# First attention of a graph network kernel: values weighed four slots at a time instead of two

## The chip, the cores and the metric

The kernel runs on one core of one Trainium2 chip. The metric is the device time of one execution in microseconds (us); the kernel before was run three times and the median counts. Beside these runs there is one execution recorded by the hardware profiler, from which all rows below come.

## The reference

Four layers of a graph network over 6250 nodes of 256 features and 106250 edges, each with a layer norm and a residual. The change touches the first one, a dot-product attention over the edges:

```
h = max(layernorm(x), 0)
q, k, v = h @ Wq + bq, h @ Wk + bk, h @ Wv + bv       # 8 heads of 32
scores = sum(q[src] * k[dst], over a head) / sqrt(32)
e = exp(scores - max of the scores of the same dst)
out = segment_sum(v[src] * e / sum(e), by dst)
x = x + out
```

The other three layers (a gated graph layer, a relational convolution with 8 edge types, an attention with additive scores and a batch norm) are not touched.

## The kernel before

Edges are sorted by destination and cut into slots of 128 edges, one edge to a partition; a slot's edges all end in one tile of 128 nodes. There are 880 slots, worked on in 55 iterations `j` of a ring of 16 slots (`RING`), each in two halves `h` of 8 slots (`GROUP`). One half is called a group here: 110 groups.

`dot_attention` is the stage of the first attention. Each engine has its own program, and they meet at semaphores only. For each group:

- GpSimd gathers for each slot the rows of its sources (`gather`, L729): per edge 256 numbers of q and then 8 heads of 32 values plus one place for the weight, 33 numbers a head. A slot of the ring is gathered anew once its sum is done.
- TensorE multiplies the transposed one-hot matrices of two slots (a pair, q = 0 to 3) with the keys of the node tile (`keys_of`, L961), which gives each edge the key of its destination. VectorE multiplies it with the q part of the rows, in place (`multiply_keys`, L1108, 512 numbers on each partition), and after four pairs sums them by head to scores (`sum_scores`, L1113).
- TensorE turns the scores (`turn_scores`, L969 and L970), VectorE scans them for running maxima by destination (`scan_within` L1121, `join_slots` L1128 to L1136, `scan_across` L1143 and L1145), with short steps of TensorE between (`row_of_ends` L979, `spread_bounds` L984, `lowered_node` L998 and L999, `differences` L990 and L991). ScalarE takes the exponential and writes the weights into the 33rd places (`weights_of`, L1079).
- VectorE weighs the values with them, in place (`weigh_values`, L1160, 2 slots x 8 heads x 32 = 512 numbers).
- TensorE sums a slot's values and weights by destination with the one-hot matrix (`sums_of`, which calls `aggregate`, L764), and VectorE adds the sum to the node tile's (`add`, which calls `accumulate`, L771). `lower_sums` (L1152) scales the running sums by the fall of the maximum.

TensorE also computes fillers (`keep_busy`, `keep_warm`, L862), whose results nobody reads; six of them stand before `turn_scores`.

The order on each engine is written out by hand in `on_vector` and `on_tensor`: in the loop over groups, group g is weighed and summed while the keys and scores of group g + 1 (`more`) are computed, and the one-hots of group g + 2 (`later`) are turned. An instruction that waits holds back all behind it on its engine. The semaphores around the change: `weight_ready` (weights written), `msg_ready` (values weighed, counted in pairs, eight to an iteration), `agg_done` (a slot summed), `acc_done` (a slot's sum added), `key_ps` and `pair_used` (keys of a pair computed, and used). The two helpers that sums and additions go through wait like this:

```python
def aggregate(pe, j, b, at, width, banks=(6, 7)):
    pe.wait_ge(acc_done, now(j, b - len(banks), RING))
    nc.tensor.matmul(psum[:, banks[b % len(banks)], 0:width], oh[:, b // GROUP, b % GROUP],
                     rows[:, b, at:at + width], start=True, stop=True).then_inc(agg_done, 1)

def accumulate(dve, j, b, place, width, banks=(6, 7), sums=acc):
    dve.wait_ge(agg_done, now(j, b, RING))
    dve.wait_ge(acc_done, now(j, b - 1, RING))
```

In this stage there are four banks for the sums. A matmul of 32-bit numbers shows as two instructions in the trace, so four L764 are the sums of two slots and four L961 the keys of one pair.

Of the kernel before, what the change touches and what calls it, by code (L numbers as in the profile page):

```python
# [18 lines left out]
ALU, ACT, AX = mybir.AluOpType, mybir.ActivationFunctionType, mybir.AxisListType  # L19
# [3 lines left out]
P = 128  # L23
N, D, HEADS, DH, RELS, EDGES = 6250, 256, 8, 32, 8, 106250
# [57 lines left out]
def build(nc, ctx, a, out):  # L82
# [3 lines left out]
    def sem(name):  # L86
        return ctx.enter_context(nc.semaphore(name))
# [65 lines left out]
    def landed(use):  # L153

        return 16 * (use + 2)
# [8 lines left out]
    def now(i, p, n=2):  # L166


        return n * i + p + n + 1
# [591 lines left out]
# [9 lines that stand above are left out]
        to = at_place(sums, place, width)  # L770
        nc.vector.tensor_tensor(to, to, psum[:, banks[b % len(banks)], 0:width], ALU.add).then_inc(acc_done, 1)  # L771
# [8 lines left out]
    shifted, weight_ready, msg_ready = sem("shifted"), sem("weight_ready"), sem("msg_ready")  # L780
# [83 lines left out]
    def dot_attention():  # L864
# [51 lines left out]
        def nth(j, h):  # L916

            return 2 * j + h + 1

        def group_rows(h):  # L920
            return rows[:, h * GROUP:(h + 1) * GROUP, :]

        def value_heads(h):
            return group_rows(h)[:, :, vat:vat + ACCW].rearrange("p s (h d) -> p s h d", d=HW)
# [76 lines left out]
        def sums_of(pe, j, h, slots):  # L1001
            pe.wait_ge(wide_ready, nth(j, h))
            for s in slots:
                if s % 2 == 0:
                    pe.wait_ge(msg_ready, now(j, 4 * h + s // 2, 8))
                aggregate(pe, j, h * GROUP + s, vat, ACCW, banks)

        def on_tensor(pe):
# [94 lines left out]
        def multiply_keys(dve, j, h, q):  # L1103
            for b in range(2):
                dve.wait_ge(ring[h * GROUP + 2 * q + b], landed(j))
            dve.wait_ge(key_ps, now(j, 4 * h + q, 8))
            pair = group_rows(h)[:, 2 * q:2 * q + 2, 0:D]
            nc.vector.tensor_tensor(pair, ps_pair(q).rearrange("p (s f) -> p s f", s=2), pair,  # L1108
                                    ALU.mult).then_inc(pair_used, 1)

        def sum_scores(dve, j, h):
            dve.wait_ge(pair_used, now(j, 4 * h + 3, 8))
            nc.vector.tensor_reduce(score[h].rearrange("p (h s) -> p s h", s=GROUP),  # L1113
                                    group_rows(h)[:, :, 0:D].rearrange("p s (h d) -> p s h d", h=HEADS),
                                    axis=AX.X, op=ALU.add).then_inc(score_ready, 1)
# [36 lines left out]
            c.step(nc.vector.scalar_tensor_tensor(acc0, ps_alpha.unsqueeze(2).to_broadcast([P, HEADS, HW]), 1.0, acc0,  # L1152
                                                  ALU.add, ALU.mult))

        def weigh_values(dve, j, h, q):
            if q == 0:
                dve.wait_ge(weight_ready, now(j, h))
            pair = value_heads(h)[:, 2 * q:2 * q + 2]
            val = pair[:, :, :, 0:DH]
            nc.vector.tensor_tensor(val, val, pair[:, :, :, DH:].to_broadcast([P, 2, HEADS, DH]),  # L1160
                                    ALU.mult).then_inc(msg_ready, 1)

        def add(dve, j, h, s, places):
            accumulate(dve, j, h * GROUP + s, places[s], ACCW, banks)

        def begin(dve, c):
            v = nc.vector
            dve.wait_ge(sums_clear, 1)
            for h in range(2):
                c.step(v.memset(by_link(link[h][:, 0:HEADS * LINK])[:, :, 0], -BIG))  # L1170
                c.step(v.memset(link[h][:, HEADS * LINK:], -BIG))
                c.step(v.memset(padded[h], 0.0))
                c.step(v.memset(breaks16[h][:, P:], 0.0))
            c.step(v.memset(bound[1], -BIG))
            c.step(v.memset(minus, -1.0))
            c.step(v.tensor_copy(flipped, ident[:, ::-1]))
            c.step(v.tensor_copy(paired[:, 0::2], ident[:, GH:]))
            c.step(v.tensor_copy(paired[:, 1::2], ident[:, 0:GH]))
            c.step(v.tensor_scalar(negated, ident[:, 0:GH], -1.0, None, ALU.mult))
            c.then(v.tensor_copy(ident16, ident[:, :]))  # L1180
            dve.sem_inc(begun, 1)

        def on_vector(dve):
            c = v_own.bind(dve)
            begin(dve, c)
            for q in range(4):
                multiply_keys(dve, 0, 0, q)
            sum_scores(dve, 0, 0)
            scan_within(dve, 0, 0)
            join_slots(dve, c, 0, 0)  # L1190
            scan_across(dve, c, 0, 0)
            multiply_keys(dve, 0, 1, 0)
            places = acc_places(slot(0, 0), GROUP)
            for g, (j, h) in enumerate(groups):
                more, later = at(g + 1), at(g + 2)
                lower_sums(dve, c, j, h, places[0])
                weigh_values(dve, j, h, 0)
                c.wait()
                if more:
                    multiply_keys(dve, *more, 1)  # L1200
                weigh_values(dve, j, h, 1)
                weigh_values(dve, j, h, 2)
                add(dve, j, h, 0, places)
                if more:
                    multiply_keys(dve, *more, 2)
                weigh_values(dve, j, h, 3)
                add(dve, j, h, 1, places)
                add(dve, j, h, 2, places)
                if more:
                    multiply_keys(dve, *more, 3)  # L1210
                    sum_scores(dve, *more)
                add(dve, j, h, 3, places)
                add(dve, j, h, 4, places)
                if more:
                    scan_within(dve, *more)
                add(dve, j, h, 5, places)
                if more:
                    join_slots(dve, c, *more)
                add(dve, j, h, 6, places)
                if more:  # L1220
                    scan_across(dve, c, *more)
                add(dve, j, h, 7, places)
                if later:
                    multiply_keys(dve, *later, 0)
                if more:
                    places = acc_places(slot(*more), GROUP)
            dve.wait_ge(acc_done, now(ITERS - 1, RING - 1, RING))
# [1541 lines left out]
```

## Time and profile before

| | us |
|---|---|
| median of three runs | 8025.69 |
| lowest and highest run | 8011.5 and 8032.68 |
| profiled execution, its time | 8034.18 |
| profiled execution, span from first to last instruction | 8031.9 |
| TensorE busy (matmuls) | 6812.9 (85%) |
| VectorE busy | 5413.0 (67%) |
| GpSimd busy | 4516.3 (56%) |
| ScalarE busy | 1518.2 (19%) |

The profile page gives busy times over the whole span, with stages that have different limits. The first attention is the stretch from about 600 to 2170 us. PE is TensorE (PEld its weight loads), DVE VectorE, ACT ScalarE, POOL GpSimd. PEclk is the granted TensorE clock as a share of full speed: 1.00 is 2.4 GHz, 0.50 is 1.2 GHz, and a value between is a mean over the stretch. The rows of the trace that are used stand in the section after the change.

### The profile page before, as it was taken

How to read it: one execution, taken by the hardware profiler on the slowest of the kernel's cores; microseconds unless marked ns; L12 is line 12 of the kernel's file. 1: busy time of each engine (PE TensorE's matmuls, PEld its weight loads, DVE VectorE, ACT ScalarE, POOL GpSimd, SP SyncE). 2: the span in 40 equal slices, each digit the busy share in tenths (PEclk: the TensorE clock that was granted, in tenths of full speed). 3: DMA queues.
4: the chain of work that ended last, by engine and by line, in shares of the span. 5: the costliest groups of instructions: out<-in, count | busy, mean ns of one | idle time of the engine just before them, and what ended most of it. 6: DMA issues, size and time to landing. Idle time of an engine off the chain costs nothing. (4 is left out here: it accounts for less than half of the span.)

```text
span 8031.9 us, 101344 instructions
## 1 busy us (share of the span) xinstructions
PE 6812.9 (85%) x30971; PEld 3926.6 (49%) x30971; DVE 5413.0 (67%) x12509; ACT 1518.2 (19%) x4812; POOL 4516.3 (56%) x4616
## 2 busy tenths in 40 slices
PE   1379999999859999899999999989999868888883
PEld 1136666666535444455555544444444444444442
DVE  8788999999876666644444444444444488888887
ACT  0021111111110000000000045500000044444441
POOL 1005555555457777777777711167777636666660
PEclk9999999999979999999999999999999999999997
DMA  0256666666643333354444544433333444444443
GB/s 8 56 204 174 173 172 171 173 172 173 165 133 101 96 98 98 99 118 135 131 130 132 135 146 162 162 114 104 103 105 103 103 142 115 114 114 113 114 110 99
DMA packets 462335, 1016.96 MB, mean 127 GB/s; under 512 B 114227, under 2 KB 229471, under 8 KB 455158
## 3 DMA queue, kind: packets, MB, share of 16 engines
q0 software_dynamic: 240960, 702.53, 32.7%
q1 hardware_dynamic: 220854, 308.06, 11.9%
q8 instruction: 258, 4.23, 0.2%
q14 instruction: 263, 2.15, 0.1%
HBM read 849.27 MB, written 160.73 MB: 126 GB/s over the span
## 5 line engine op out<-in xcount | busy, mean ns | idle before, releaser
L764 PE MATMUL psum<-rows,oh 128*128 128x257 f32 (+2 forms) x8800 | 2708.4, 406 | 362.8 <-DMA rows<-h_tab,src_i 119.0
L862 PE MATMUL psum<-ident,ones 128*128 128x512 bf16 x9419 | 2516.8, 381 | 0.0
L771 DVE TENSOR_TENSOR acc<-acc,psum 128x264 f32 (+2 forms) x3520 | 1480.6, 421 | 1143.3 <-PE psum L764 1065.0
L764 PEld LDWEIGHTS psum<-rows,oh 128*128 128x128 f32 x8800 | 1497.5, 190 | 1322.2 <-issue 421.0
L729 POOL DMA_INDIRECT rows<-qv_tab,src_i x880 | 872.3, 991 | 1241.4 <-SPq L2706 560.0
L862 PEld LDWEIGHTS psum<-ident,ones 128*128 128x128 bf16 x9419 | 912.4, 99 | 820.3 <-issue 14.3
L729 POOL DMA_INDIRECT rows<-xh_tab,src_i x880 | 835.0, 949 | 613.4 <-PE psum L764 312.9
L729 POOL DMA_INDIRECT rows<-h_tab,src_i x880 | 912.6, 1037 | 291.2 <-issue 242.5
L729 POOL DMA_INDIRECT rows<-h_tab,wts x880 | 875.3, 995 | 268.1 <-issue 241.0
L729 POOL DMA_INDIRECT rows<-hw_tab,rel_i x880 | 857.3, 974 | 283.8 <-issue 222.1
L771 DVE TENSOR_TENSOR kh<-kh,psum 128x257 f32 x880 | 371.6, 422 | 634.8 <-PE psum L764 631.5
L961 PE MATMUL psum<-kh,oht 128*128 x1760 | 475.0, 392 | 7.0 <-ACT oht L1055 1.2
L599 PE MATMUL psum<-acc,rows 128*128 128x512 f32 (+1 forms) x1000 | 401.3, 556 | 0.5 <-ACT rows L2242 0.5
L961 PEld LDWEIGHTS psum<-kh,oht 128*128 128x128 f32 x1760 | 318.1, 191 | 71.3 <-issue 23.6
L1108 DVE TENSOR_TENSOR rows<-psum,rows 128x512 f32<-128x512 f32 x440 | 301.0, 684 | 28.1 <-PE psum L961 15.9
L2152 POOL TENSOR_TENSOR rows<-rows 128x256 f32<-128x256 f32 x50 | 32.3, 646 | 503.5 <-DMA rows<-x_tab 454.3
L577 ACT ACTIVATE rows<-rows 128x1 f32<-128x1 f32 x200 | 40.7, 203 | 1353.4 <-DVE rows L1608 1248.9
L1160 DVE TENSOR_TENSOR rows<-rows 128x512 f32<-128x512 f32 x440 | 292.3, 685 | 1.0 <-ACT rows L1079 1.0
L599 PEld LDWEIGHTS psum<-acc,rows 128*128 128x128 f32 x1000 | 186.4, 190 | 206.5 <-issue 203.1
L1498 DVE TENSOR_TENSOR rows<-rows 128x512 f32<-128x512 f32 x440 | 283.8, 686 | 4.5
L756 DVE TENSOR_TENSOR oh<-iota_row,dl 128x1024 f32<-128x1024 f32 x220 | 268.2, 1220 | 6.2 <-ACTq L2706 3.8
L1113 DVE TENSOR_REDUCE wts<-rows 128x64 f32<-128x2048 f32 x110 | 251.7, 2288 | 3.8
(393 smaller groups left out, 7314.1 us busy)
## 6 DMA issues: line engine op xcount, KB each, us to landing
wts<-hots SPq DMA_DIRECT2D x220, 256.0 KB
hw_tab<-acc SPq DMA_DIRECT2D x50, 1024.0 KB, 4.1
part_tab<-rows SPq DMA_DIRECT2D x50, 512.0 KB
rows<-part_tab SPq DMA_DIRECT2D x50, 512.0 KB, 5.3
hots<-oh SPq DMA_DIRECT2D x74, 256.0 KB, 2.7
rows<-qv_tab,src_i POOLq DMA_INDIRECT x880, 3.7
rows<-h_tab,src_i POOLq DMA_INDIRECT x880, 2.8
rows<-h_tab,wts POOLq DMA_INDIRECT x880, 2.8
```

Of the source, the lines that this page charges most:

```text
L577: nc.scalar.activation(sd[p], ve[p], ACT.Sqrt).then_inc(std_ready, 1)
L599: mm = nc.tensor.matmul(to, ht[p][:, k * P:(k + 1) * P], w[:, k * width + at:k * width + at + size], start=k == 0, stop=bias is None and k ...
L729: nc.gpsimd.indirect_dma_start(rows[:, b, 0:width], None, table, bass.IndirectOffsetOnAxis(index, 0)).then_inc(ring[b], 16)
L756: nc.vector.tensor_tensor(to[:, h], iota_row[:, :].unsqueeze(1).to_broadcast([P, GROUP, P]), local[:, bass.ds(s0 + h * GROUP, GROUP)].unsq ...
L764: nc.tensor.matmul(psum[:, banks[b % len(banks)], 0:width], oh[:, b // GROUP, b % GROUP], rows[:, b, at:at + width], start=True, stop=True ...
L771: nc.vector.tensor_tensor(to, to, psum[:, banks[b % len(banks)], 0:width], ALU.add).then_inc(acc_done, 1)
L862: nc.tensor.matmul(bank, ones[:, :].bitcast(BF16)[:, 0:P], busy, start=True, stop=True)
L961: mm = nc.tensor.matmul(ps_pair(q)[:, b * D:(b + 1) * D], oht[:, h, 2 * q + b], at_place(kh, places[2 * q + b], D), start=True, stop=True)
L1108: nc.vector.tensor_tensor(pair, ps_pair(q).rearrange("p (s f) -> p s f", s=2), pair, ALU.mult).then_inc(pair_used, 1)
L1113: nc.vector.tensor_reduce(score[h].rearrange("p (h s) -> p s h", s=GROUP), group_rows(h)[:, :, 0:D].rearrange("p s (h d) -> p s h d", h=HE ...
L1160: nc.vector.tensor_tensor(val, val, pair[:, :, :, DH:].to_broadcast([P, 2, HEADS, DH]), ALU.mult).then_inc(msg_ready, 1)
L1498: nc.vector.tensor_tensor(val, val, pair[:, :, :, DH:].to_broadcast([P, 2, HEADS, DH]), ALU.mult).then_inc(msg_ready, 1)
```

## The change

VectorE's four `weigh_values` of a group, each over two slots, become two over four slots each. Each of the two raises `msg_ready` by 2, so that it still counts pairs. TensorE waits for it only ahead of slots 0 and 4, and for all four slots then. In VectorE's order for a group, the addition of slot 0 stands ahead of the second weighing instead of behind the third, the second weighing (slots 4 to 7) stands ahead of the keys of q = 2, and nothing stands between these keys and the addition of slot 1.

```diff
--- before.py
+++ after.py
@@ -1001,8 +1001,8 @@
         def sums_of(pe, j, h, slots):
             pe.wait_ge(wide_ready, nth(j, h))
             for s in slots:
-                if s % 2 == 0:
-                    pe.wait_ge(msg_ready, now(j, 4 * h + s // 2, 8))
+                if s % 4 == 0:
+                    pe.wait_ge(msg_ready, now(j, 4 * h + s // 2 + 1, 8))
                 aggregate(pe, j, h * GROUP + s, vat, ACCW, banks)
 
         def on_tensor(pe):
@@ -1152,13 +1152,13 @@
             c.step(nc.vector.scalar_tensor_tensor(acc0, ps_alpha.unsqueeze(2).to_broadcast([P, HEADS, HW]), 1.0, acc0,
                                                   ALU.add, ALU.mult))
 
-        def weigh_values(dve, j, h, q):
-            if q == 0:
+        def weigh_values(dve, j, h, half):
+            if half == 0:
                 dve.wait_ge(weight_ready, now(j, h))
-            pair = value_heads(h)[:, 2 * q:2 * q + 2]
-            val = pair[:, :, :, 0:DH]
-            nc.vector.tensor_tensor(val, val, pair[:, :, :, DH:].to_broadcast([P, 2, HEADS, DH]),
-                                    ALU.mult).then_inc(msg_ready, 1)
+            four = value_heads(h)[:, 4 * half:4 * half + 4]
+            val = four[:, :, :, 0:DH]
+            nc.vector.tensor_tensor(val, val, four[:, :, :, DH:].to_broadcast([P, 4, HEADS, DH]),
+                                    ALU.mult).then_inc(msg_ready, 2)
 
         def add(dve, j, h, s, places):
             accumulate(dve, j, h * GROUP + s, places[s], ACCW, banks)
@@ -1198,12 +1198,10 @@
                 c.wait()
                 if more:
                     multiply_keys(dve, *more, 1)
+                add(dve, j, h, 0, places)
                 weigh_values(dve, j, h, 1)
-                weigh_values(dve, j, h, 2)
-                add(dve, j, h, 0, places)
                 if more:
                     multiply_keys(dve, *more, 2)
-                weigh_values(dve, j, h, 3)
                 add(dve, j, h, 1, places)
                 add(dve, j, h, 2, places)
                 if more:
```

## Rows read from the trace of the kernel before

**Rows 1.** stretch, its us, busy PE, PEld, DVE, ACT, POOL, granted clock, DMA share, GB/s

```profile
1000.00:2000.00 1000.00, 940.68 (x4798) 640.07 (x4798) 914.66 (x1838) 188.28 (x425) 558.55 (x564) 1.00 0.63 172
612.00:626.00 14.00, 10.89 (x36) 8.15 (x37) 8.30 (x17) 2.20 (x6) 5.85 (x7) 0.63 0.48 140
```

**Rows 2.** one line's instructions, ns min/median/max, first and last start, forms

```profile
L1160 DVE TENSOR_TENSOR rows<-rows x440: 680/684/714, 621.2 to 2168.8; 128x512 f32<-128x512 f32 x147
...
L756 DVE TENSOR_TENSOR oh<-iota_row,dl x220: 1210/1218/1286, 2293.8 to 6375.6; 128x1024 f32<-128x1024 f32 x110
```

**Rows 3.** VectorE in order of time, one group: start us, us, instruction, count

```profile
1402.08 0.69 DVE L1160 TENSOR_TENSOR rows<-rows 128x512 f32<-128x512 f32 x1
1402.92 0.69 DVE L1108 TENSOR_TENSOR rows<-psum,rows 128x512 f32<-128x512 f32 x1
1403.53 1.28 DVE L1160 TENSOR_TENSOR rows<-rows 128x512 f32<-128x512 f32 x2
1404.73 0.42 DVE L771 TENSOR_TENSOR acc<-acc,psum 128x264 f32 x1
1405.07 0.68 DVE L1108 TENSOR_TENSOR rows<-psum,rows 128x512 f32<-128x512 f32 x1
1405.67 0.68 DVE L1160 TENSOR_TENSOR rows<-rows 128x512 f32<-128x512 f32 x1
1406.27 0.95 DVE L771 TENSOR_TENSOR acc<-acc,psum 128x264 f32 x2
1407.15 0.68 DVE L1108 TENSOR_TENSOR rows<-psum,rows 128x512 f32<-128x512 f32 x1
1407.86 2.29 DVE L1113 TENSOR_REDUCE wts<-rows 128x64 f32<-128x2048 f32 x1
```

**Rows 4.** waits, 1000 to 2000 us: us in total, times, longest; VectorE, then TensorE

```profile
DVE psum L1131 <- PE psum L979: 46.5, 71, 1.0
DVE rows L1108 <- PE psum L961: 4.0, 26, 0.2
...
PE psum L969 <- DVE wts L1113: 32.7, 70, 0.8
```

**Rows 5.** TensorE in order of time, same group, then one row of ScalarE's

```profile
1401.66 1.13 PE L961 MATMUL psum<-kh,oht 128*128 x4
1402.88 1.13 PE L764 MATMUL psum<-rows,oh 128*128 128x264 f32 x4
1403.85 1.03 PE L961 MATMUL psum<-kh,oht 128*128 x4
...
1405.60 1.03 PE L961 MATMUL psum<-kh,oht 128*128 x4
...
1408.30 1.46 PE L862 MATMUL psum<-ident,ones 128*128 128x512 bf16 x6
1410.21 0.49 PE L969 MATMUL psum<-wts 128*128 128x128 f32 x2 [0.45 <-DVE wts L1113]
...
1401.76 0.29 ACT L1079 ACTIVATE rows<-psum 128x64 f32<-128x64 f32 x1 [1.94 <-PE psum L991]
```

**Rows 6.** order of time elsewhere: two of VectorE, TensorE's start, a standing start

```profile
380.12 1.22 DVE L664 TENSOR_TENSOR oht<-iota_row,dl 128x1024 bf16<-128x1024 f32 x1
381.25 0.16 DVE L581 RECIPROCAL rows<-rows 128x1 f32<-128x1 f32 x1
...
622.68 1.97 PE L764 MATMUL psum<-rows,oh 128*128 128x264 f32 x4
...
2601.42 0.67 PE L764 MATMUL psum<-rows,oh 128*128 128x257 f32 x2 [0.60 <-DVE acc L771]
...
2602.13 0.42 DVE L771 TENSOR_TENSOR acc<-acc,psum 128x257 f32 x1 [0.33 <-PE psum L764]
```

**Rows 7.** GpSimd in order of time, and from issue to landing of transfers into rows

```profile
1413.30 1.01 POOL L729 DMA_INDIRECT rows<-qv_tab,src_i  x1 [0.73 <-PE psum L764]
...
DMA to landing us min/median/max: 3.4/3.7/5.1
```

## The prediction

> **What bounds the kernel now.** The reading starts with the stretches: from 1000 to 2000 us, well inside the first attention, TensorE shows 94% busy, VectorE 91%, GpSimd 56%, and the granted clock is 1.00, the level of 2.4 GHz [rows 1]. Both leading engines are nearly full, so the share says nothing of which one sets the pace. In 1000 us VectorE starts 283 weighings, four for each group of eight slots, which makes about 71 groups; over the whole stage 440 of them start between 621.2 and 2168.8 us [rows 2]. The last starts 3.6 us into its own group (1405.67 against 1402.08 in [rows 3]), so one group takes (2168.8 - 3.6 - 621.2) / 109 = 14.17 us. The stage is a loop of 110 nearly identical groups, and whatever the change does is done some 109 times: 0.1 us a group is 11 us, or 0.14% of the kernel. About 24 us, 0.3%, is what a measurement of this kernel can tell from no change; that is 0.22 us a group.
>
> Next come VectorE's instructions in order of time over one group [rows 3] and its waits [rows 4]. VectorE works without a pause but for two places. One is L1131, which waits for TensorE's row of ends (46.5 us in 71 waits, 0.65 us each). The other is the multiplication of keys q=1 at 1402.92, 0.15 us after the weighing before it has ended; only 26 of these 71 waits are recorded. TensorE's own row [rows 5] shows the opposite view: it too runs from one step to the next, and its one true pause is 0.45 us before it turns the scores at 1410.21, waiting for the reduction (70 waits, 32.7 us in [rows 4]). In front of that pause stand six filler multiplications (L862), which end at 1408.30 + 1.46 = 1409.76. So each engine is behind the other at some point of the group, and only the order of the hand-overs tells what a change is worth.
>
> **The hand-overs around the edit.** Before: the first weighing runs from 1402.08 to 1402.77, and TensorE's sums of slots 0 and 1 start at 1402.88, 0.11 us after it [rows 3, 5]. They could have begun earlier: the keys of q=1 were started at 1401.66, and where nothing is waited for the next step begins 0.97 us or less after (1402.88 to 1403.85). From there TensorE runs sums 0 and 1, keys q=2 (1403.85), sums 2 and 3, and keys q=3 (1405.60 to 1406.63), with no wait in between: 3.75 us from the first sum to the end of the last keys. VectorE takes those keys at 1407.15, that is 0.52 us after they are done. The lag it needs is 0.13 us: keys q=1 end at 1401.66 + 1.13 = 1402.79 and are taken at 1402.92. TensorE therefore has 0.52 - 0.13 = 0.39 us of slack at this point, and no more.
>
> **What the change does on VectorE.** It takes out four instructions of 512 elements and puts in two of 1024. The old kind takes 0.684 us (median of 440). The new shape is not in the trace; the nearest row is L756, the same operation on as many elements in the same memory, also with a broadcast operand: 1.218 us, from 1.210 to 1.286 [rows 2]. I take 1.22. What the engine's own row pays is less than these durations, since starts overlap: 0.60 us from one 512 start to the next (1405.07 to 1405.67, [rows 3]), and 1.13 us behind a 1024 one (380.12 to 381.25, [rows 6]). One merged pair saves 2 x 0.60 - 1.13 = 0.07 us, two pairs 0.14 us a group, 15 us in all, if VectorE set the pace. The 0.24 us by which keys q=1 stand later than 0.60 us after the first weighing (0.84 less 0.60) would vanish too, as the longer weighing covers that wait. VectorE's own sum from the first weighing to keys q=3 would be 1.13 + 0.60 + 0.34 (addition 0) + 1.13 + 0.60 + 0.53 + 0.35 (additions 1 and 2, which wait for each other) = 4.68 us, against 5.07 us in the rows (1402.08 to 1407.15): 0.39 us less.
>
> **What it does on TensorE.** The first sum now waits for four slots to be weighed instead of two. The weighing starts where it did, since nothing in front of it changes: ScalarE's weights end at 1401.76 + 0.29 = 1402.05 [rows 5]. It ends at 1402.08 + 1.22 = 1403.30, and the sums start 0.11 us later, at 1403.41, which is 0.53 us after 1402.88. TensorE stands still for those 0.53 us, and all that is queued behind that wait on it moves by as much: keys q=2, sums 2 and 3, keys q=3, the turning of the next one-hots, sums 4 to 6 and the fillers. None of them finds a wait that would absorb it: sums 4 need the second half weighed, which happens by 1405.7, and bank freed by addition 0. Keys q=3 end at 1406.63 + 0.53 = 1407.16, and VectorE can take them at 1407.29.
>
> **Which is later.** Addition 0 now stands ahead of the second weighing, and needs slot 0's sum. The row nearest to a slot summed from a standing start is 2601.42 to the addition's start at 2602.13, 0.71 us [rows 6]. So addition 0 starts at 1403.41 + 0.71 = 1404.12; VectorE is free for it at 1402.08 + 1.13 + 0.60 = 1403.81 and waits 0.31 us. Then 0.34, the weighing 1.13, keys q=2 at 1405.59 (TensorE has them at 1404.88 + 0.53 + 0.13 = 1405.54), 0.60, 0.53 and 0.35: VectorE is ready for keys q=3 at 1407.07. TensorE offers them at 1407.29. The later of the two counts, and it is 0.14 us after the 1407.15 of now. The 0.39 us that VectorE saves is turned into waiting, 0.31 us at addition 0 and 0.2 us at keys q=3.
>
> **Behind that point** the order is unchanged: the reduction, the scores turned on TensorE, the row of ends, the scans, keys q=0, the factor, the weighing. It all hangs on the reduction and moves by 0.14 us. One cover shrinks: the reduction ends at 1407.86 + 2.29 = 1410.15 and TensorE turns the scores at 1410.21; with +0.14 that is 1410.35, while the fillers in front of it end at 1409.76 + 0.53 = 1410.29. Of 0.45 us of pause 0.06 remains. GpSimd's gathers wait for the sums of the slot they refill. The last one of a half is issued at 1413.30 and lands a median 3.7 us (at most 5.1) later [rows 7], about 1418 to 1419.4, and is needed at keys q=3 of the next group, 1407.15 + 14.17 = 1421.3; the first slots' gathers move by 0.53 us and have more room. No DMA comes onto the path. SyncE's loads hang on TensorE's and ScalarE's marks and have a whole group's room.
>
> **The sum.** +0.14 us x 109 = +15 us. Ends: with the weighing at 1.210 us and a lag of 0.11 us in place of 0.13, +0.11 us (12 us); with 1.286 us, +0.21 us (23 us). The profiled execution becomes 8031.9 + 15 = 8047 us of span, and 8034.18 + 15 = 8049 us of time. The median of the runs lies 8.5 us below that execution, at 8025.69, and the forecast is 8025.69 + 15 = 8041 us.
>
> The Trainium skill, Trace Analysis, section Optimizing Scalar/DVE Operations, has one rule for the change and one against it. Larger operations help throughput where the engine is saturated, and it gives about 60 ns of overhead per VectorE operation on SBUF; the 0.07 us of my rows agrees, and by this rule alone the change would bring the gain of the first rival below. It also says that where VectorE causes bubbles on other engines, breaking instructions up lets work finish sooner; read backwards this is the forecast, and the rows side with it, since TensorE's start at 1402.88 hangs on the end of the short weighing.
>
> **Rivals.** (1) VectorE sets the pace throughout and TensorE catches up somewhere. For it: VectorE's unbroken row and its 91%. Against: the 3.75 us of TensorE steps hold no wait to shrink. If everything of it holds, -0.39 x 109 = -42 us, 7983 us; if only the wait at addition 0 stays, 1407.07 against 1407.15, -9 us, 8017 us. (2) On the slow side: the four-slot instruction with its strided rows saves nothing of the fixed part. If it lasts as long as two overlapped ones (1.28 us, 1403.53 in [rows 3]), keys q=3 come 0.20 us later, +22 us; if 2 x 0.684 = 1.37 us, +0.29 us a group, +31 us, 8057 us. Past 1.30 us of duration it is slower by more than 0.3%. Against it: the strided 512 weighing costs what the dense L1108 does. (3) The 0.06 us left before the scores are turned is gone, because TensorE loses more than 0.53 us at its new pause; every further 0.1 us is +11 us, so about +26 us, 8052 us. (4) The new pause costs TensorE its clock. In 612 to 626 us the granted clock is 0.63 with TensorE waiting a lot [rows 1], and the same sums take 1.97 us in place of 1.13 [rows 5, 6]: 0.84 us for each of four steps, 3.4 us a group, and if it happened in one group of ten, +37 us, 8063 us. Against it: 0.45 us pauses in every group leave 1.00 now, and the change moves a pause more than it adds one.
>
> **How the numbers follow.** Forecast 0.68, rival 1 0.09, rival 2 0.12, rival 3 0.07, rival 4 0.04. The likeliest case's own range is +12 to +23 us, and the three runs of before spread over 21 us, so about 8028 to 8058. The range over all cases leaves out the fast half of rival 1 and the far ends of 2 and 4: 8022 to 8061 us. Slower by over 0.3% (from +24 us): most of rivals 2 to 4 (0.16) and 0.08 of the forecast through its upper end and scatter, 0.24. Faster: 0.05, from rival 1. Within 0.3%: 0.71.
>
> **What the profile after would show.** One group 14.3 us long. L1160 at 1.22 us, twice a group. TensorE's L764 with a new pause of about 0.5 us before slot 0; additions (L771) waiting about 0.3 us for L764 once a group; L1108 waiting about 0.2 us for L961 at q=3, and no longer at q=1; the wait of TensorE for L1113 down from 0.45 us to near nothing; L1131's wait unchanged. VectorE's busy time in the stage falls by 110 x (4 x 0.684 - 2 x 1.22) = 33 us, with no gain from it. The prediction is wrong if L1108 at q=3 follows the additions without a wait, or if the weighing lasts 1.3 us.

## The result and the profile after

| | before | after |
|---|---|---|
| median of the runs, us | 8023.64 (6 runs) | 8052.86 (6 runs) |
| lowest and highest run, us | 8011.5 and 8032.68 | 8048.41 and 8058.51 |
| profiled execution, span, us | 8031.9 | 8048.5 |
| TensorE busy, us | 6812.9 | 6796.9 |
| VectorE busy, us | 5413.0 | 5410.4 |

The changed kernel is 0.33% slower: the ratio of its time to that of before is 1.0033, with a 95% interval of 1.0022 to 1.0043, or 18 to 35 us. The forecast was 8041 us with a range of 8022 to 8061. The six runs of before are the three on which the forecast was built and three more.

Single executions of one kernel lie 10 to 34 us apart in these runs, so the length of the loop itself is the finer measure: the first and the last start of one instruction of it, 110 of which stand one group apart. Before, then after (duration min/median/max in ns, first and last start in us):

```profile
L1143 DVE TENSOR_TENSOR_SCAN wts<-wts,psum x110: 469/477/478, 618.5 to 2164.4; 64x128 f32<-64x128 bf16 x110
```

```profile
L1143 DVE TENSOR_TENSOR_SCAN wts<-wts,psum x110: 466/477/477, 610.9 to 2180.7; 64x128 f32<-64x128 bf16 x110
```

Before, 2164.4 - 618.5 = 1545.9 us; after, 2180.7 - 610.9 = 1569.8 us. The loop is 23.9 us longer, 0.219 us for each of its 109 steps. The median of the 109 steps goes from 14.15 to 14.37 us. Outside it the two executions differ by 7.6 us ahead of the loop, in favour of the changed one, and by 0.3 us behind it (8031.9 - 2164.4 = 5867.5 against 8048.5 - 2180.7 = 5867.8). So all of the loss that belongs to the change lies in the loop.

The stretch from 1000 to 2000 us after (columns as in [rows 1], which has it before) and the weighings (as in [rows 2]):

```profile
1000.00:2000.00 1000.00, 925.44 (x4722) 630.20 (x4722) 901.03 (x1669) 185.57 (x419) 531.64 (x555) 1.00 0.62 169
...
L1160 DVE TENSOR_TENSOR rows<-rows x220: 1216/1222/1227, 613.1 to 2186.0; 128x1024 f32<-128x1024 f32 x110
```

Both leading engines are less busy than before, 93% and 90% in place of 94% and 91%: neither got more work, both wait more. The granted clock is 1.00 as before. The waits in the same stretch, VectorE's and then TensorE's (us in total, times, longest; [rows 4] before):

```profile
DVE psum L1131 <- PE psum L979: 46.1, 69, 1.0
DVE acc L771 <- PE psum L764: 15.6, 70, 0.2
DVE rows L1108 <- PE psum L961: 0.5, 1, 0.5
...
PE psum L764 <- ACT oh L1060: 48.8, 70, 1.0
PE psum L969 <- DVE wts L1113: 0.6, 2, 0.4
```

TensorE has a new wait ahead of the sums, 70 times 0.7 us, and has lost the one ahead of the scores (32.7 us, now 0.6). The view names ScalarE's copy L1060 as the one waited for; that copy ends at 1405.55 + 1.04 = 1406.59 in the group below, while the sums start at 1407.15, so it is the weighing that came last. VectorE waits for the sum of slot 0 (15.6 us in 70 waits).

One group in order of time (start, us), VectorE ([rows 3] before):

```profile
1405.39 0.41 DVE L1152 SCALAR_TENSOR_TENSOR acc<-psum,acc 128x264 f32 x1
1405.82 1.23 DVE L1160 TENSOR_TENSOR rows<-rows 128x1024 f32<-128x1024 f32 x1
1406.96 0.68 DVE L1108 TENSOR_TENSOR rows<-psum,rows 128x512 f32<-128x512 f32 x1
1407.87 0.43 DVE L771 TENSOR_TENSOR acc<-acc,psum 128x264 f32 x1 [0.22 <-PE psum L764]
1408.22 1.22 DVE L1160 TENSOR_TENSOR rows<-rows 128x1024 f32<-128x1024 f32 x1
1409.35 0.68 DVE L1108 TENSOR_TENSOR rows<-psum,rows 128x512 f32<-128x512 f32 x1
1409.95 0.95 DVE L771 TENSOR_TENSOR acc<-acc,psum 128x264 f32 x2
1411.03 0.69 DVE L1108 TENSOR_TENSOR rows<-psum,rows 128x512 f32<-128x512 f32 x1
1411.76 2.29 DVE L1113 TENSOR_REDUCE wts<-rows 128x64 f32<-128x2048 f32 x1
```

TensorE and ScalarE in the same group ([rows 5] before):

```profile
1404.60 0.43 PE L990 MATMUL psum<-wts,ident 128*128 128x64 f32 x2
...
1405.33 1.13 PE L961 MATMUL psum<-kh,oht 128*128 x4
1407.15 1.13 PE L764 MATMUL psum<-rows,oh 128*128 128x264 f32 x4 [0.69 <-ACT oh L1060]
1408.11 1.03 PE L961 MATMUL psum<-kh,oht 128*128 x4
...
1409.87 1.03 PE L961 MATMUL psum<-kh,oht 128*128 x4
...
1412.57 1.46 PE L862 MATMUL psum<-ident,ones 128*128 128x512 bf16 x6
1414.10 0.49 PE L969 MATMUL psum<-wts 128*128 128x128 f32 x2
...
1405.43 0.28 ACT L1079 ACTIVATE rows<-psum 128x64 f32<-128x64 f32 x1 [1.93 <-PE psum L991]
1405.55 1.04 ACT L1060 CAST oh<-wts 128x1024 f32<-128x1024 bf16 x1
```

The first weighing runs from 1405.82 to 1407.05, the sums start at 1407.15, the last keys end at 1409.87 + 1.03 = 1410.90, and VectorE takes them at 1411.03, 0.13 us later. Its second addition starts 0.53 us behind the first, at 1410.48, and would have let it go on at 1410.83: it waits 0.20 us there. A group lasts from 1405.82 to the same weighing at 1420.19: 14.37 us.

From the first weighing to the keys q=3 it is 5.21 us, in place of 5.07. From the scan across (L1145) before the weighing to the weighing it is 1405.82 - 1404.07 = 1.75 us; before, with that scan at 1400.39, it was 1.69. One group shows such small steps only to 0.01 or 0.02 us, so they are better taken over all 109 groups of the trace: on the mean the first piece grew by 0.14 us, the second by 0.07 (medians 1.69 and 1.76), the step from the keys to the reduction by 0.01, and the rest of the group not at all. Together they are the 0.22 us.

### The profile page after: what moved, and what is told of

Its sections match the earlier page's. It is cut to its first block and busy times, and to the rows that moved or that the text cites. A ratio compares the mean times of both kernels' runs of the same rounds, so it can differ in the third digit from the quotient of the medians.

```text
span 8048.5 us, 101124 instructions
## 1 busy us (share of the span) xinstructions
PE 6796.9 (84%) x30971; PEld 3918.3 (49%) x30971; DVE 5410.4 (67%) x12289; ACT 1518.1 (19%) x4812; POOL 4485.6 (56%) x4616
## 3 DMA queue, kind: packets, MB, share of 16 engines
q0 software_dynamic: 240960, 702.53, 32.7%
## 5 line engine op out<-in xcount | busy, mean ns | idle before, releaser
L729 POOL DMA_INDIRECT rows<-qv_tab,src_i x880 | 844.6, 960 | 1285.2 <-PE psum L764 558.5
L961 PEld LDWEIGHTS psum<-kh,oht 128*128 128x128 f32 x1760 | 317.9, 190 | 71.5 <-issue 23.9
L2150 POOL TENSOR_TENSOR rows<-rows 128x256 f32<-128x256 f32 x50 | 32.7, 654 | 506.4 <-DMA rows<-x_tab 487.1
L1496 DVE TENSOR_TENSOR rows<-rows 128x512 f32<-128x512 f32 x440 | 283.5, 686 | 4.4
L1160 DVE TENSOR_TENSOR rows<-rows 128x1024 f32<-128x1024 f32 x220 | 268.8, 1222 | 3.1 <-issue 0.7
```

The lines of the kernel that those rows point to most:

```text
L729: nc.gpsimd.indirect_dma_start(rows[:, b, 0:width], None, table, bass.IndirectOffsetOnAxis(index, 0)).then_inc(ring[b], 16)
L961: mm = nc.tensor.matmul(ps_pair(q)[:, b * D:(b + 1) * D], oht[:, h, 2 * q + b], at_place(kh, places[2 * q + b], D), start=True, stop=True)
L1160: nc.vector.tensor_tensor(val, val, four[:, :, :, DH:].to_broadcast([P, 4, HEADS, DH]), ALU.mult).then_inc(msg_ready, 2)
```

## Experiments

Theory A is that of the prediction: TensorE's wait for four weighed slots delays what stands behind it, and the keys q=3 come too late for VectorE. Theory B: the cost lies on VectorE, in the longer instruction or the new order. "Loop" is the time from the first to the last scan within the loop, measured as above in the profiled execution of each kernel; "group" is it divided by 109, and "median step" the median of the 109 distances between the starts of the scan across (L1145 before). A few long groups make the mean larger than the median; the kernel with the wait alone has two kinds of group. Each ratio is to executions of the kernel before made alongside, whose medians were 8020.5 to 8025.3 us.

| kernel | loop, us | group, us | median step, us | median, us (runs) | ratio to before, 95% |
|---|---|---|---|---|---|
| before | 1545.9 | 14.18 | 14.15 | 8023.64 (6) | 1 |
| changed | 1569.8 | 14.40 | 14.37 | 8052.86 (6) | 1.0033 (1.0022 to 1.0043) |
| pairs, TensorE waits for four | 1570.7 | 14.41 | 14.37 | 8045.81 (7) | 1.0029 (1.0015 to 1.0042) |
| pairs, TensorE waits for two | 1518.2 | 13.93 | 13.91 | 7999.31 (10) | 0.9968 (0.9954 to 0.9981) |
| two pairs, then four | 1511.3 | 13.86 | 13.84 | 7984.87 (6) | 0.9953 (0.9938 to 0.9968) |
| changed, keys in the pause | 1547.3 | 14.20 | 14.16 | 8020.93 (10) | 0.9996 (0.9985 to 1.0007) |
| changed, seven fillers | 1570.2 | 14.41 | 14.37 | 8044.11 (8) | 1.0028 (1.0017 to 1.0039) |
| changed, half heads | 1573.0 | 14.43 | 14.37 | 8042.00 (10) | 1.0027 (1.0017 to 1.0037) |
| changed, more VectorE work | 1572.9 | 14.43 | 14.37 | 8042.83 (10) | 1.0026 (1.0017 to 1.0036) |
| row of ends first | 1494.7 | 13.71 | 13.68 | 7974.21 (4) | 0.9931 (0.9907 to 0.9955) |
| row of ends first, places read early | 1450.2 | 13.30 | 13.27 | 7926.99 (4) | 0.9883 (0.9867 to 0.9900) |
| before, with the wait alone | 1784.9 | 16.38 | 15.52 or 17.11 | 8256.59 (4) | 1.0289 (1.0272 to 1.0306) |

### The instruction apart from the wait

```diff
-            four = value_heads(h)[:, 4 * half:4 * half + 4]
-            val = four[:, :, :, 0:DH]
-            nc.vector.tensor_tensor(val, val, four[:, :, :, DH:].to_broadcast([P, 4, HEADS, DH]),
-                                    ALU.mult).then_inc(msg_ready, 2)
+            for q in (2 * half, 2 * half + 1):
+                pair = value_heads(h)[:, 2 * q:2 * q + 2]
+                val = pair[:, :, :, 0:DH]
+                nc.vector.tensor_tensor(val, val, pair[:, :, :, DH:].to_broadcast([P, 2, HEADS, DH]),
+                                        ALU.mult).then_inc(msg_ready, 1)
```

> The changed kernel's order and TensorE's wait for four weighed slots, but each weighing as two instructions of two slots back to back. Theory (the wait is the cost, the form of the instruction is not): the fourth slot is weighed 0.60 + 0.68 = 1.28 us after the first weighing starts in place of 1.22, so TensorE's sums, the last keys and the group come 0.06 us later than by the wait of the changed kernel, less the 0.07 us by which its four-slot instruction started late: a group of 14.35 to 14.40 us as in the changed kernel (14.37), some 20 to 28 us over the kernel before. Rival (the four-slot instruction or VectorE's load is the cost): the group falls back to the 14.15 us of before or under it.

Measured: a loop of 1570.7 us, as long as the changed kernel's. The merged instructions are gone and the loss has stayed, so it is not theirs. Two small effects cancel here: the first pair starts 0.07 us sooner than the merged instruction did (1.69 us behind the scan across in place of 1.76), and the second pair ends later, so that weighing to keys q=3 takes 5.28 us in place of 5.21 (medians).

The second kernel adds to this one the old wait of TensorE:

```diff
-                if s % 4 == 0:
-                    pe.wait_ge(msg_ready, now(j, 4 * h + s // 2 + 1, 8))
+                if s % 2 == 0:
+                    pe.wait_ge(msg_ready, now(j, 4 * h + s // 2, 8))
```

> As the first run of this call, but TensorE waits for each pair as in the kernel before. Theory: TensorE starts its sums 0.11 us after the first pair is weighed, its keys q=3 are ready at the same distance as before, and VectorE sets the pace; the second weighing now fills the 0.24 us in which VectorE waited for keys q=1, so a group takes 14.15 - 0.24 = 13.91 us and the kernel is 26 us faster than before. Rival (VectorE's order or load is the cost): about as slow as the changed kernel, 14.3 us or more.

Measured: 1518.2 us, 52.5 us less than with the wait for four and 27.7 less than before. In this pair of kernels VectorE does the same instructions in the same order; only the wait differs. TensorE in the kernel that waits for four, and then in the one that waits for two:

```profile
1412.18 1.13 PE L764 MATMUL psum<-rows,oh 128*128 128x264 f32 x4 [0.69 <-ACT oh L1060]
```

```profile
1405.08 0.49 PE L969 MATMUL psum<-wts 128*128 128x128 f32 x2 [0.21 <-DVE wts L1113]
...
1411.90 1.13 PE L764 MATMUL psum<-rows,oh 128*128 128x264 f32 x4
```

With the wait for two the sums have no recorded wait ahead of them, and the pause ahead of the scores is back, 0.21 us. So the change carried a gain in its order on VectorE: with the second pair weighed right behind the first, VectorE no longer waits for keys q=1 (the median step fell by the 0.24 us that were forecast for it). The longer wait on TensorE took more than that away.

### What merging is worth where nobody waits

The third kernel, shown against the second, has the two pairs for slots 0 to 3 and one instruction for slots 4 to 7, for all of which TensorE waits ahead of slot 4:

```diff
-                if s % 2 == 0:
-                    pe.wait_ge(msg_ready, now(j, 4 * h + s // 2, 8))
+                if s in (0, 2):
+                    pe.wait_ge(msg_ready, now(j, 4 * h + s // 2, 8))
+                if s == 4:
+                    pe.wait_ge(msg_ready, now(j, 4 * h + 3, 8))
@@
-            for q in (2 * half, 2 * half + 1):
-                pair = value_heads(h)[:, 2 * q:2 * q + 2]
-                val = pair[:, :, :, 0:DH]
-                nc.vector.tensor_tensor(val, val, pair[:, :, :, DH:].to_broadcast([P, 2, HEADS, DH]),
-                                        ALU.mult).then_inc(msg_ready, 1)
+            for first, count in ((0, 2), (2, 2)) if half == 0 else ((4, 4),):
+                some = value_heads(h)[:, first:first + count]
+                val = some[:, :, :, 0:DH]
+                nc.vector.tensor_tensor(val, val, some[:, :, :, DH:].to_broadcast([P, count, HEADS, DH]),
+                                        ALU.mult).then_inc(msg_ready, count // 2)
```

> As the second run, with slots 4 to 7 weighed by one instruction of four slots (nobody waits for the first of them early). Theory: merging is worth its 0.07 us where TensorE does not wait for it: a group of 13.84 us, 34 us faster than the kernel before. Rival (merged instructions cost more than they save): slower than the second run.

Measured: 1511.3 us, 6.9 us less than with pairs alone, 0.063 us a group for one merged pair (0.07 by the median step). VectorE around it:

```profile
1412.19 1.22 DVE L1163 TENSOR_TENSOR rows<-rows 128x1024 f32<-128x1024 f32 x1
1413.33 0.68 DVE L1110 TENSOR_TENSOR rows<-psum,rows 128x512 f32<-128x512 f32 x1
```

The next instruction starts 1.14 us after the merged one; two pairs take 1.20 (1413.25 to 1414.45 in the kernel with pairs alone).

### TensorE's pause filled

The changed kernel with the keys q=2 ahead of the sums:

```diff
                     keys_of(pe, *more, 1, places)
-                sums_of(pe, j, h, range(0, 2))
-                if more:
                     keys_of(pe, *more, 2, places)
-                sums_of(pe, j, h, range(2, 4))
+                sums_of(pe, j, h, range(0, 4))
```

> The changed kernel with one change on TensorE: the keys q=2 stand ahead of the sums of slots 0 and 1, so that they fill the pause of 0.6 us before the sums. Theory: TensorE offers the keys q=3 some 0.9 us earlier, VectorE no longer waits for them and sets the pace: a group of about 14.05 us, 35 us faster than the changed kernel and 11 us faster than before. Rival (the pause is harmless, the cost lies on VectorE): 14.37 us, as the changed kernel.

Measured: 1547.3 us, 22.5 less than the changed kernel. The direction is that of theory A; the size is two thirds of the forecast. VectorE and then TensorE:

```profile
1411.41 0.41 DVE L1150 SCALAR_TENSOR_TENSOR acc<-psum,acc 128x264 f32 x1
1411.84 1.23 DVE L1158 TENSOR_TENSOR rows<-rows 128x1024 f32<-128x1024 f32 x1
...
1413.89 0.43 DVE L771 TENSOR_TENSOR acc<-acc,psum 128x264 f32 x1 [0.22 <-PE psum L764]
...
1416.84 0.68 DVE L1106 TENSOR_TENSOR rows<-psum,rows 128x512 f32<-128x512 f32 x1
...
1405.75 0.49 PE L969 MATMUL psum<-wts 128*128 128x128 f32 x2 [0.72 <-DVE wts L1111]
...
1411.34 1.99 PE L961 MATMUL psum<-kh,oht 128*128 x8
1413.17 2.01 PE L764 MATMUL psum<-rows,oh 128*128 128x264 f32 x8
```

The keys q=3 now start right behind the additions and TensorE has 0.72 us of pause ahead of the scores: VectorE sets the pace here. A group takes 14.16 us where 14.05 were forecast, and most of the missing 0.11 us is on VectorE itself: the weighing starts 0.43 us behind L1152 in place of 0.36, 0.07 us late. The addition of slot 0 still waits, as late as in the changed kernel (2.05 us behind the weighing's start): TensorE cannot begin the sums before all four slots are weighed.

### How much cover was left on each side

Two small additions to the changed kernel, one on each engine: a seventh filler ahead of the scores, and a memset on VectorE ahead of the keys q=3.

```diff
-                    keep_busy(pe, *more, 2, 6)
+                    keep_busy(pe, *more, 2, 7)
```

> The changed kernel with seven fillers in place of six before the scores are turned. In the kernel before this place had a pause of 0.45 us, in the changed one 0.05 us. Theory (the change used this cover up): one filler of 0.22 us now lengthens each group by 0.17 to 0.22 us, 19 to 24 us in all over the changed kernel. Rival (TensorE still has room there): no change, 14.37 us a group.

Measured: 1570.2 us against 1569.8. Nothing, where 19 to 24 us were expected. TensorE in this kernel:

```profile
1405.00 1.67 PE L862 MATMUL psum<-ident,ones 128*128 128x512 bf16 x7
1406.53 0.49 PE L969 MATMUL psum<-wts 128*128 128x128 f32 x2
```

The fillers' modelled end is 1406.67, yet the scores are started at 1406.53, 0.06 us after the reduction (1404.18 + 2.29 = 1406.47). A modelled end is later than the moment from which the next matmul can start: seven fillers hold TensorE for at most 1.53 us, not 1.67. The cover that I had put at 0.06 us was at least a whole filler. The rows of the weight loads (PEld) show this room better than those of the matmuls: ahead of L969 they stand idle 0.96 us a group before (67.2 us in 70 waits), 0.57 in the changed kernel (39.6 in 69) and 0.36 with seven fillers (25.4 in 70), from 1000 to 2000 us. How much of the 0.36 could still be filled was not tried.

```diff
+        spare = place_of(128, count=1)[0]
@@
                 add(dve, j, h, 2, places)
+                nc.vector.memset(spare, 0.0)
                 if more:
                     multiply_keys(dve, *more, 3)
```

> The changed kernel with one more instruction on VectorE, a memset of 128 numbers that nobody reads, between addition 2 and the keys q=3; it should take 0.1 to 0.2 us of VectorE. Theory (VectorE waits for TensorE at the keys q=3 by about 0.2 us): no change, within 0.05 us a group. Rival (VectorE sets the pace of the changed kernel): each group 0.1 to 0.2 us longer, 11 to 22 us in all.

Measured: 1572.9 us, 3.1 us over the changed kernel, 0.03 us a group, where the memset takes 0.17 us:

```profile
1403.17 0.95 DVE L771 TENSOR_TENSOR acc<-acc,psum 128x264 f32 x2
1404.10 0.17 DVE L1208 MEMSET wts<- 128x128 f32 x1
1404.25 0.69 DVE L1109 TENSOR_TENSOR rows<-psum,rows 128x512 f32<-128x512 f32 x1
```

The steady groups are unchanged (1399.04 to 1413.41 is 14.37 us from weighing to weighing, and so is the median step); the 3.1 us lie in a few long groups. VectorE has spare time at this point, as theory A says.

### Why the weighing starts late

The changed kernel with each weighing as two instructions over four slots and four heads:

```diff
-            four = value_heads(h)[:, 4 * half:4 * half + 4]
-            val = four[:, :, :, 0:DH]
-            nc.vector.tensor_tensor(val, val, four[:, :, :, DH:].to_broadcast([P, 4, HEADS, DH]),
-                                    ALU.mult).then_inc(msg_ready, 2)
+            for k in range(2):
+                four = value_heads(h)[:, 4 * half:4 * half + 4, 4 * k:4 * k + 4]
+                val = four[:, :, :, 0:DH]
+                nc.vector.tensor_tensor(val, val, four[:, :, :, DH:].to_broadcast([P, 4, HEADS // 2, DH]),
+                                        ALU.mult).then_inc(msg_ready, 1)
```

> The changed kernel with each weighing as two instructions of 512 numbers, each over four slots and four heads in place of two slots and eight heads. It asks why the first four-slot weighing starts 0.10 us after ScalarE's weights, where the two-slot one starts 0.03 us after. If the reach over four slots does it, the start stays at 0.10 us and a group takes 14.37 + 0.07 = 14.44 us; if the 1024 numbers do it, the start falls to 0.03 us and the group takes 14.37 us, as with two instructions of two slots.

Measured: 1573.0 us. The start falls back to 0.36 us behind L1152 (0.04 us after ScalarE's weights end at 1399.94 + 0.28 = 1400.22):

```profile
1399.90 0.41 DVE L1152 SCALAR_TENSOR_TENSOR acc<-psum,acc 128x264 f32 x1
1400.26 1.29 DVE L1161 TENSOR_TENSOR rows<-rows 128x512 f32<-128x512 f32 x2
```

The loop is 3.2 us over the changed kernel's, the median step 14.37 us as in it. So it is the size of 1024 numbers that goes with the late start, not the reach over four slots. Only the weighing behind the wait for ScalarE starts late: the other merged one, in the kernel with two pairs and then four, starts 0.33 us behind the start of the addition, as other instructions do. Why is open. It costs nothing on top of pairs in sum, since two pairs end 0.06 us later than one instruction of four.

### The wait alone

The kernel before, with TensorE's wait for four slots and nothing else changed:

```diff
-                if s % 2 == 0:
-                    pe.wait_ge(msg_ready, now(j, 4 * h + s // 2, 8))
+                if s % 4 == 0:
+                    pe.wait_ge(msg_ready, now(j, 4 * h + s // 2 + 1, 8))
```

> The kernel before with TensorE's wait of the changed kernel and nothing else: four weighings of two slots in the old order, but the sum of slot 0 waits for slots 0 to 3. In the old order the second weighing ends at 1404.21, so the sums start at 1404.32 in place of 1402.88, 1.44 us later. Theory (late sums cost what exceeds the slack of the first taker behind them): the keys q=2 are ready 1.44 us later, VectorE had 0.06 us of slack there, and the third weighing and two additions stand behind them; a group takes 14.15 + 1.38 = 15.53 us, 150 us more in all. Rival (TensorE has room to catch up, and only its last 0.39 us of slack or less counts, or the wait is harmless): 15.2 us or less.

Measured: 8256.59 us, 16.38 us a group. The sum was right for one kind of group and there are two kinds. From the weighing at 1364.81 to the one at 1380.34 it is 15.53 us, the number forecast; from 1412.92 to 1430.00 it is 17.08. The granted clock tells them apart (columns as in [rows 1]), and below it stand TensorE's sums of both kinds, and the keys of the second:

```profile
1352.00:1367.00 15.00, 12.86 (x67) 8.60 (x66) 12.62 (x27) 2.67 (x6) 7.67 (x8) 1.00 0.56 155
1402.00:1418.00 16.00, 13.95 (x66) 9.40 (x66) 12.89 (x26) 2.67 (x6) 7.62 (x8) 0.92 0.48 136
...
1367.05 1.13 PE L764 MATMUL psum<-rows,oh 128*128 128x264 f32 x4 [1.53 <-issue]
...
1415.16 1.83 PE L764 MATMUL psum<-rows,oh 128*128 128x264 f32 x4 [1.53 <-issue]
1416.78 1.91 PE L961 MATMUL psum<-kh,oht 128*128 x4
```

After the pause of 1.53 us the four matmuls of the sums take 1.13 us at the granted 1.00 and 1.83 in a stretch where it is 0.92, and the keys 1.91 in place of 1.03. The 0.92 is a mean: from 1417 to 1418 us the granted clock is 0.50, the lower level of 1.2 GHz, and from 1419 us on it is 1.00 again, all within one group. The 17.08 us are 1.55 more than 15.53. Counted by their first sums, 52 of the 109 groups kept the full clock (median 15.52 us) and 57 did not (17.11). Groups of one kind follow each other, 2 to 13 at a time. The pause ahead of the sums is 1.52 or 1.53 us in groups of both kinds, so the pause alone does not decide which group is hit; what else does is open.

In the changed kernel the new pause of 0.69 us in each group left the granted clock at 1.00 from 1000 to 2000 us.

### A version faster than both

VectorE sets the pace once the wait is for two slots, and its largest remaining wait is the one for the row of ends (48.0 us in 72 waits from 1000 to 2000 us, 0.67 each; L1133 in this kernel). TensorE computes that row behind the keys q=0. The third kernel, with TensorE's order changed there:

```diff
+                sums_of(pe, j, h, range(7, 8))
+                if more:
+                    row_of_ends(pe, *more)
                 if later:
                     places = places_of(*later)
                     keys_of(pe, *later, 0, places)
                 if more:
-                    row_of_ends(pe, *more)
-                sums_of(pe, j, h, range(7, 8))
-                if more:
-                    keep_busy(pe, *more, 3, 2)
+                    keep_busy(pe, *more, 3, 1)
                     spread_bounds(pe, *more)
```

> The version with two pairs and then four slots, and on TensorE the sum of slot 7 and the row of ends ahead of the next keys q=0 (and one filler fewer behind them, so that the bounds are not held up). Theory (VectorE sets the pace, but for its wait of 0.66 us for the row of ends at L1133): the row is started as soon as the scan within is done in place of behind 1.03 us of keys, so the wait shrinks by some 0.47 us: a group of 13.84 - 0.47 = 13.37 us, 85 us faster than the kernel before. Rival (TensorE is as full as VectorE and what is moved ahead holds up something else): 13.7 us or more.

Measured: 1494.7 us, 51.2 under before, but only 0.15 us a group of the 0.47 expected. VectorE no longer waits for the row, but for the bounds (25.9 us in 72 waits from 1000 to 2000 us), and TensorE shows why:

```profile
1409.64 0.16 DVE L1133 TENSOR_TENSOR psum<-psum,wts 1x8 f32<-1x8 f32 x1
...
1411.59 0.48 DVE L1145 TENSOR_TENSOR_SCAN wts<-wts,psum 64x128 f32<-64x128 bf16 x1 [0.35 <-PE psum L984]
...
1409.16 0.38 PE L979 MATMUL psum<-wts 128*1 128x128 f32 x2
1409.91 1.10 PE L961 MATMUL psum<-kh,oht 128*128 x4 [0.38 <-issue]
...
1411.16 0.40 PE L984 MATMUL psum<-ones,wts 1*64 1x1 f32 x4
```

Between the row and the keys TensorE stands 0.38 us on its own issue. What the program has there is the reading of the key places into registers. In the kernel before it stood behind the turning of the scores (L970), and the keys q=0 started 0.05 us after the shown end of those matmuls. The last kernel moves it ahead of the fillers:

```diff
                 sums_of(pe, j, h, range(4, 7))
+                if later:
+                    places = places_of(*later)
                 if more:
                     keep_busy(pe, *more, 2, 6)
@@
                 if later:
-                    places = places_of(*later)
                     keys_of(pe, *later, 0, places)
```

> The version with the row of ends first, with TensorE's reading of the key places moved from between the row of ends and the keys q=0 to ahead of the six fillers. In the version before it a group took 13.67 us in place of the 13.37 forecast: TensorE stood for 0.38 us (its own issue) before the keys q=0, its bounds (L984) came late and VectorE waited 0.35 us for them. Theory (the reading of the places is that 0.38 us): the keys start right behind the row of ends, the wait at L1145 goes, and a group takes 13.3 to 13.4 us, some 85 us faster than the kernel before. Rival (TensorE is simply full behind the row of ends): no change, 13.67 us.

Measured: 7926.99 us, 0.9883 of before, 13.27 us a group in the steady stretch (1400.56 to 1413.83). The keys start without a gap behind the row, and VectorE is 96% busy:

```profile
1409.60 0.38 PE L979 MATMUL psum<-wts 128*1 128x128 f32 x2
1409.90 1.13 PE L961 MATMUL psum<-kh,oht 128*128 x4
...
1000.00:2000.00 1000.00, 970.03 (x5043) 670.31 (x5044) 963.59 (x1883) 201.48 (x454) 589.37 (x601) 1.00 0.66 184
```

## Why the prediction was right, point by point

**What bounds the kernel.** Right: the order of the hand-overs tells, and the busy shares do not. Both engines' shares fell while the kernel got slower.

**The size of the weighing.** 1.22 us forecast from the row of the same shape elsewhere, 1.222 measured. Rival 2, that the merged instruction saves nothing, falls: it is 0.06 us shorter than two pairs (1.22 against 1.28).

**TensorE's start.** Forecast 0.53 us later behind the weighing, measured (1407.15 - 1405.82) against (1402.88 - 1402.08), 1.33 against 0.80: 0.53. The new pause shows as 0.69 us, not the 0.5 forecast, because TensorE already stood 0.09 us at this place and the weighing itself starts 0.07 us late. The keys q=3 are taken 0.13 us after they end, as forecast, and the piece from the weighing to them grew by 0.14 us, as forecast. The pair of kernels that differ in the wait alone shows that this is the cause.

**The start of the weighing.** This is the term that was mis-sized. The prediction says "The weighing starts where it did, since nothing in front of it changes". It starts 0.07 us later, counted from the scan before it, which is 8 us over the loop, and the step between the keys and the reduction took 0.01 us more, another 1. The prediction put this term at nothing because the order in front of it is unchanged, and no run here shows why a merged weighing starts late. With these the 15 us become the 24 of the loop. The forecast of 8041 lies 12 us under the median of 8052.86; 9 of them are these terms, and the remaining 3 are inside the scatter of the runs, which spread over 21 us before. The chance of 0.71 was on "within 0.3%". The measured 0.33% lies just outside, where the chance was 0.24, and its interval (0.22 to 0.43) takes in both.

**Waits of VectorE.** About 0.3 us for slot 0's sum and 0.2 for the keys q=3 were forecast. Measured: the addition starts 0.91 us behind the keys q=1 in place of 0.60, so 0.31 in the row (0.22 of it recorded as a wait), and 0.20 for the keys.

**VectorE's busy time.** A fall of 33 us was forecast. The page shows 2.6 us less over the whole span, and per group it is 12.94 us before and 12.95 after (914.66 and 901.03 us in 1000 us, at 14.15 and 14.37 us a group). Taking durations for busy time was wrong, since the stretch in which one instruction overlaps the next counts once. That the two new waits give back what the merging saves would fit, but was not tested. No time hangs on it.

**The pause before the scores.** It shrank from 0.45 us to almost nothing, as forecast, but reading this as cover used up was wrong. Rival 3 was priced with 0.06 us left, and a whole filler more cost nothing. That rival 3's 8052 us is nearest to the measured time is chance: its mechanism, the used-up cover, did not act.

**Rival 1**, VectorE sets the pace: against it speak the two kernels with all four pairs, and the memset that is free. Its price of -42 us, VectorE's saving without TensorE's delay, was near to what VectorE has to give: with TensorE's wait back at two slots the same order on VectorE is 27.7 us under before, and one merged pair gives another 6.9, 34.6 in all. Merging the first two pairs as well was not tried without the delay.

**Rival 4**, the clock: it did not come with the new pause of 0.69 us. With 1.53 us it did, in 57 of 109 groups, at about 1.6 us each.

## What to carry to other kernels

Before two instructions are merged, look who waits for the first of them: the merged one saves its overhead (0.06 us here) on its own engine, and delays the first user by the length of the second half (0.53 us here). Merge those whose first part nobody awaits, and keep the early ones small. The Trainium skill, Perfetto Trace Analysis, section Optimizing Scalar/DVE Operations, names both sides: larger operations where VectorE is saturated, and smaller ones where it is not but holds up other engines. Here the trace agrees with both, by 0.06 us for the one (slots 4 to 7) and 0.53 us for the other (slots 0 to 3). The prediction gives the second rule without its condition, and with VectorE 91% busy the condition does not settle this case; who waits for the first part does. When two engines are both nearly full, count the slack at each hand-over; a fix on one side shows only when the other's wait is not made longer by it.

## What the runs showed of the hardware

- A weighing of 1024 numbers that waits for ScalarE started 0.10 us after ScalarE's end, one of 512 numbers 0.03 us after it (medians over 109 groups; the first in the changed kernel and the three others that keep the merged first weighing, the second in the eight kernels with pairs or half heads). Behind an addition of its own engine there was no such difference (0.33 to 0.35 us from start to start). The cause is open.
- A matmul's modelled end lies after the time from which the next can start: a seventh filler of 0.21 us fitted into a pause that showed as 0.07 us.
- Where TensorE paused 1.53 us once a group, 57 of 109 groups ran in part at the lower clock level (0.50 from 1417 to 1418 us in the group shown), with the granted clock back at 1.00 within the same group.
- TensorE's reading of slot places into registers showed as 0.38 us of issue time once only the row of ends stood in front of it.
